# First layer's recurrence: the last sum of the read-out moves from GpSimd and VectorE to TensorE

## The reference

```python
def _step(Sm, inputs):
    q_t, k_t, v_t, beta_t = inputs
    Sk = jnp.einsum('bhde,bhe->bhd', Sm, k_t)
    delta = v_t - Sk
    Sm = Sm + beta_t[..., None] * jnp.einsum('bhd,bhe->bhde', delta, k_t)
    o_t = jnp.einsum('bhde,bhe->bhd', Sm, q_t)
    return (Sm, o_t)
...
return outputs @ Wo + bo
```

## Time and profile before

| | |
|---|---|
| device time, median of 3 runs | 4969.15 us |
| lowest and highest | 4963.04, 4973.53 us |
| span of the profiled execution | 4960.9 us |
| PE / DVE / ACT / POOL busy over the span | 77% / 73% / 51% / 60% |
| PEld busy over the span | 35% |

### The profile page before, as it was taken

How to read it: one execution, slowest core, us unless ns; L and a number is a source line. 1 busy time by engine, 2 the same in 40 slices (tenths; PEclk the granted TensorE clock), 3 DMA queues, 4 the chain that set the end, 5 groups by cost and what they waited for, 6 DMA issues and landing times. The chain is left out here.

```text
span 4960.9 us, 46627 instructions
## 1 busy us (share of the span) xinstructions
PE 3814.6 (77%) x13222; PEld 1745.4 (35%) x13222; DVE 3629.3 (73%) x5288; ACT 2514.6 (51%) x3881; POOL 2956.4 (60%) x2245
## 2 busy tenths in 40 slices
PE   5444565999649978888787799998978777777776
PEld 2111223754226633333333454553423222222222
DVE  7999774134547679999998544545543899999998
ACT  4444431344538856666664344444355555555554
POOL 4888465027254479999993211114420798889987
PEclk7777788999869999999999898989989999899998
DMA  1110211112211144444441432321100444444342
GB/s 50 43 43 9 84 38 55 68 57 76 97 56 58 43 143 156 154 154 157 156 152 62 89 43 38 42 34 48 61 9 34 142 134 141 134 138 140 129 141 98
DMA packets 161698, 434.77 MB, mean 88 GB/s; under 512 B 28150, under 2 KB 51384, under 8 KB 160048
## 3 DMA queue, kind: packets, MB, share of 16 engines
q1 hardware_dynamic: 142512, 374.41, 24.7%
q0 software_dynamic: 18944, 57.57, 3.3%
HBM read 363.67 MB, written 68.68 MB: 87 GB/s over the span
## 5 line engine op out<-in xcount | busy, mean ns | idle before, releaser
L1673 ACT ACTIVATE mb_h<-m_dt,m_a_neg 128x512 f32<-128x512 f32 x1024 | 665.0, 681 | 724.0 <-DVE r L1828 332.8
L1532 PE MATMUL mb_y<-r,m_diag_y 128*128 128x512 f32 x1024 | 546.9, 669 | 275.8 <-POOL r L1753 164.8
L1819 DVE TENSOR_TENSOR_SCAN mb_h<-mb_h,m_u 128x1024 f32<-128x1024 f32 x320 | 734.0, 2294 | 10.4
L1776 POOL TENSOR_TENSOR m_u<-m_bsb,m_xs 128x1024 f32<-128x1024 f32 x256 | 599.9, 2366 | 175.7 <-DMA m_bsb<-bc_rows 175.7
L1776 POOL TENSOR_TENSOR m_u<-m_bsb,m_dtx 128x1024 f32<-128x1024 f32 x256 | 596.2, 2358 | 49.1 <-DVE m_dtx L1860 27.9
L1532 PE MATMUL mb_y<-m_hc,w_common 128*128 128x512 f32 x1024 | 495.3, 623 | 153.3 <-DVE m_hc L1828 87.2
L1819 DVE TENSOR_TENSOR_SCAN m_hs<-mb_h,m_u 128x1024 f32<-128x1024 f32 x192 | 437.5, 2279 | 1.7 <-POOL m_u L1776 1.7
L1532 PEld LDWEIGHTS mb_y<-r,m_diag_y 128*128 128x128 f32 x1024 | 196.1, 207 | 622.2 <-POOL r L1753 244.0
L2302 DVE TENSOR_REDUCE at_mx<-at_ps_s 128x4 f32<-128x512 f32 (+1 forms) x256 | 242.8, 957 | 233.6 <-PE at_ps_s L2116 233.6
L1753 POOL TENSOR_TENSOR r<-m_hs,m_csb 128x1024 f32<-128x1024 f32 x128 | 306.0, 2391 | 119.1 <-DVE m_hs L1819 118.5
L1532 PEld LDWEIGHTS mb_y<-m_hc,w_common 128*128 128x128 f32 x1024 | 190.4, 196 | 450.5 <-issue 191.6
(11 more groups left out here) (518 smaller groups left out, 8519.4 us busy)
## 6 DMA issues: line engine op xcount, KB each, us to landing
m_bsb<-bc_rows SPq DMA_DIRECT2D x256, 512.0 KB, 4.9
m_csb<-bc_rows SPq DMA_DIRECT2D x256, 512.0 KB, 4.0
at_q<-q_parts SPq DMA_DIRECT2D x144, 128.0 KB
x_slots<-d_zeros SPq DMA_DIRECT2D x8, 1024.0 KB, 5.0
kept_x<-r SPq DMA_DIRECT2D x2, 4096.0 KB, 14.1
xg_xg<-x_slots SPq DMA_DIRECT2D x32, 256.0 KB, 2.6
y_slots<-xg_yo POOLq DMA_DIRECT2D x32, 256.0 KB, 2.3
xl_xg<-x_slots SPq DMA_DIRECT2D x32, 256.0 KB, 2.6
```

The source lines that it names most:

```text
L1532: mm = nc.tensor.matmul(ps_y[:, h], weight, hc[:, q % RING, s], start=False, stop=g == GROUPS - 1 and s == SG - 1)
L1673: ins = nc.scalar.activation(ps_h[:, q % 2, s], dt[:, i % 2, h], ACT.Exp, scale=a_neg[:, n:n + 1])
L1776: nc.gpsimd.tensor_tensor(u[:, q % RING], bsb[:, n % RING], dtx[:, i % 2, h].unsqueeze(1).broadcast_to([P, SG, TILE]), ALU.mult).then_inc( ...
L1819: V.tensor_tensor_scan(flat(to), flat(ps_h[:, q % 2]), flat(u[:, q % RING]), 0.0, ALU.mult, ALU.add).then_inc(h_ready, 1)
```

## The change

The addition over the last index goes to TensorE. For each half of a tile, 256 outputs a partition, `sum_terms` issues eight products of the unit matrix (`w["eye"]`, stationary) with a strided view of `sq_q`: the moving operand of product `e` is element `e` of each group of eight, so its neighbouring columns lie eight float32 numbers apart. All eight add up in PSUM, in the bank of `rounding.pst`. `halve` on GpSimd and `outputs` on VectorE are gone, and so is `o_tm` in SBUF. `turn_out` now reads PSUM, and stands after pair 2 of the next tile, where it stood after pair 1. The semaphore `summed` takes the place of `o_part` and `halved`: `queries` waits for it by half tiles, and `turn_out` for both halves.

```diff
-        o_tm = sb("o_tm", [P, TILE])
...
+        o_tm = rounding.pst[:].rearrange("p (m b) c -> p m (b c)", m=2)
...
+            def sum_terms(a, m):
+                pe.wait_ge(sq_ready, a * PAIRS + (m + 1) * PAIRS // 2)
+                if a and m == 0:
+                    pe.wait_ge(o_turned, a)
+                half = STEPS // 2
+                terms = sq_q[:, m * half:(m + 1) * half].rearrange("p t h e -> p (t h) e")
+                for e in range(D0):
+                    mm = nc.tensor.matmul(o_tm[:, m], w["eye"], terms[:, :, e], start=e == 0, stop=e == D0 - 1)
+                mm.then_inc(summed, 1)
...
                 if i:
+                    sum_terms(i - 1, 1)
                     out(i - 1)
                 ffn(i)
+                sum_terms(i, 0)
+            sum_terms(NT - 1, 1)
             out(NT - 1)
...
                 if i:
-                    pool.wait_ge(o_part, (i - 1) * 4 + p // 2 + 1)
+                    pool.wait_ge(summed, (i - 1) * 2 + p // (PAIRS // 2) + 1)
...
-            def halve(i, j):
-                pool.wait_ge(sq_ready, i * PAIRS + 2 * j + 2)
-                both = sq_q[:, 4 * j:4 * j + 4].rearrange("p t h e -> p (t h) e")
-                G.tensor_tensor(both[:, :, 0:D0 // 2], both[:, :, 0:D0 // 2], both[:, :, D0 // 2:], ALU.add).then_inc(halved, 1)
...
-            def outputs(i, j):
-                dve.wait_ge(halved, i * 4 + j + 1)
-                V.tensor_reduce(o_tm[:, j * P:(j + 1) * P], sq_q[:, 4 * j:4 * j + 4].rearrange("p t h e -> p (t h) e")[:, :, 0:D0 // 2],
-                                AX, ALU.add).then_inc(o_part, 1)
...
             def turn_out(i):
-                dve.wait_ge(o_part, 4 * i + 4)
+                dve.wait_ge(summed, 2 * i + 2)
                 if i:
                     dve.wait_ge(o_projected, i)
-                V.transpose(o_fm[:], o_tm[:]).then_inc(o_turned, 1)
+                V.transpose(o_fm[:], rounding.pst[:].rearrange("p m c -> p (m c)")).then_inc(o_turned, 1)
...
-                    if p == 1 and i:
-                        outputs(i - 1, 3)
-                        turn_out(i - 1)
                     if p == 1 and more:
                         norms(i + 1)
+                    if p == 2 and i:
+                        turn_out(i - 1)
...
-                    if p in (3, 5, 7):
-                        outputs(i, p // 2 - 1)
```

More of the change, by code:

```diff
@@ L300, in delta_ffn @@
         (block, projected, evacuated, turned, sqk_ready, norm2, norm1, shifted, rn_ready, parts, m_ready, c_ready, prepared, s_gated,
-         stepped, state_ready, sq_ready, o_part, o_turned, o_projected, s_ready, h_ready, relu_ready, r2_ready, y_ready,
-         g_ready, mixed, lifted, gated, zeroed, cleared, halved, x_in0, x_in1, *rounds) = ctx.enter_context(phase(
+         stepped, state_ready, sq_ready, summed, o_turned, o_projected, s_ready, h_ready, relu_ready, r2_ready, y_ready,
+         g_ready, mixed, lifted, gated, zeroed, cleared, x_in0, x_in1, *rounds) = ctx.enter_context(phase(
              nc, "projected evacuated turned sqk_ready norm2 norm1 shifted rn_ready parts m_ready c_ready prepared s_gated "
-             "stepped state_ready sq_ready o_part o_turned o_projected s_ready h_ready relu_ready r2_ready y_ready "
-             "g_ready mixed lifted gated zeroed cleared halved x_in0 x_in1 "
+             "stepped state_ready sq_ready summed o_turned o_projected s_ready h_ready relu_ready r2_ready y_ready "
+             "g_ready mixed lifted gated zeroed cleared x_in0 x_in1 "
               "round_chain fc_ready fc_turned low1 low1s low2 proj_ready proj_turned round_done"))
@@ L526, in _ @@
                     queries(i, p)
-                    if p % 2:
-                        halve(i, p // 2)
                     if p == 0 and more:
@@ L622, in _ @@
                         turn(i + 1)
-                    if p == 1 and i:
-                        outputs(i - 1, 3)
-                        turn_out(i - 1)
                     if p == 1 and more:
                         norms(i + 1)
+                    if p == 2 and i:
+                        turn_out(i - 1)
                     if p == 2 and more:
                         inverse(i + 1)
-                    if p in (3, 5, 7):
-                        outputs(i, p // 2 - 1)
                     if p == 5 and more:
                         overlaps(i + 1)
-            outputs(NT - 1, 3)
             turn_out(NT - 1)
```

## The result

The changed kernel takes 4989.82 us, the median of 11 runs (4982.19 to 5006.19); the kernel before took 4965.99 us beside it. The ratio is 1.0059, with a 95% interval of 1.0038 to 1.0080: slower by about 29 us, where 4960.2, no measurable change, was forecast. (The medians are 23.8 us apart; the ratio is formed from the fast runs alone, without one of the kernel before at 6565.52 us.) The profiled execution has a span of 4999.2 us.

What follows compares the result with a forecast made beforehand. VectorE was taken to bound the recurrence phase. Removed work -41.3, new waits +28.6 and +0.4, and the phase's end +3.4 sum to -8.9 us: 4960.2 us from 4969.15, eight-in-ten range 4947 to 5004.

Steps and rivals of the forecast that it cites:

- I take the cheap side, as nearest: TensorE's sums: strided columns assumed to cost what columns cost now, 0.214 us an instruction, 3.42 us for eight products.
- rival A: TensorE's sums: strided columns cost twice, eight products take 6.84 us, VectorE waits 5.0 us a tile, 4998.8 us; chance 0.33.
- VectorE's and GpSimd's removed work: Recurrence tiles: 37.8 us off VectorE plus the big transposition's 3.5 us wait for GpSimd, together 41.3 us.
- the place of the wait: VectorE at the small transposition, for sums queued behind TensorE's third and fourth projection: 2.2 us in 13 tiles, 28.6 us.
- the small transposition out of PSUM: VectorE's small transposition reading PSUM instead of SBUF: cost 0, bounds -0.3 and +1.6 us over 16.
- GpSimd's wait at the big transposition: Start of each tile: the big transposition's wait for GpSimd's last product, 0.29 us in each of 12 tiles, would go.
- Rival B: TensorE stays at 2.4 GHz, sums end earlier and VectorE never waits: -39.7 us, 4929.5; chance 0.07.
- Rival C: GpSimd takes over as the bound, with about 21 of 28.5 us a tile; judged impossible, no separate chance given.

Runs made afterwards that it cites:

- e1: Changed kernel with each product reading another buffer at its own stride, output meaningless; 0.216 us an instruction at stride 1, 0.45 to 0.46 at 8.
- e2: Changed kernel with the product buffer's last index outermost, so TensorE reads neighbouring columns; ratio 0.9983 to the kernel before.
- e3: Changed kernel, strided sums kept, with the small transposition one pair later, behind pair 3 and `inverse`; ratio 0.9945 to the kernel before.
- e10: Changed kernel, strided sums kept, with `inverse` and then the small transposition behind pair 3; ratio 0.9931 to the kernel before.
- e6: Kernel before with only the small transposition moved, from behind pair 1 to behind pair 2, ahead of `inverse`; ratio 1.0022 to the kernel before.
- e8: Changed kernel with neighbouring columns, `inverse` and then small transposition behind pair 3, last half's sum split in two; 0.9898 of the kernel before, 4920.1 against 4967.81 us.
- e5: Changed kernel with the second half's sums issued ahead of the third and fourth projection on TensorE; ratio 1.0016 to the kernel before.

## Why the prediction was wrong

*The failed step* is "I take the cheap side, as nearest": 16 x 0.214 = 3.42 us for eight products that read one float32 of eight. They take 16 x 0.46 = 7.4, since a float32 read alone out of its 16 bytes costs 1.8 ns and not 0.84 (e1). Ahead of it stands the reason given, that GpSimd is indifferent to distance. For writing that is still so (e2), but the evidence was from another engine at 2.5 ns a column, and the text itself had noted so: an engine that needs 2.5 ns a column need not show a price of 1.8. The rival had a stated rule behind it, and the forecast nothing of its own: with no nearer row for the cheap end, A deserved at least even chances. The rule of 16-byte lines, cited there against the choice, was the one to follow.

*What followed from it* was rival A: a wait of 5.0 us in 13 tiles (3.6 to 5.4 measured, 4.9 in the mean), 0.8 in tile 15 (1.4), 5.1 more at the end (592.53 - 584.86 = 7.67 us where there were 2.02, so 5.7), and 4998.8 us, +29.6. Measured: +29 us, and 30.1 in the phase. One clause in it was off: the lower level does not double the price again, it stays 0.46 us an instruction.

*The rest held.* VectorE's and GpSimd's removed work, 41.3 us (the period less its wait is 33.4 - 4.9 = 28.5, as forecast); the place of the wait, behind the third and fourth projection; and the small transposition out of PSUM, 716 ns against some 711. e2 is the forecast's own case with the one wrong price put right: -8.8 us of phase against -8.9 forecast, a stall of 2.26 against 2.2, and 37.4 - 7.5 (at the end) = 29.9 us of wait in the tiles against 28.6 + 0.4. GpSimd's wait at the big transposition is gone.

*Rival B* needed TensorE not to fall to 1.2 GHz. In the changed kernel it is still at 1.00 when the third projection starts (333.46) and falls right behind that: 0.52 in the window 334 to 335. e3 and e10 show the rival's case: with the slow sums and almost no wait of VectorE, the mean clock over 200 to 300 us is 1.00, where the changed kernel has 0.91. *Rival C* didn't come: GpSimd is busy 61.5 us of 100. (Its "about 21" is 0.79 x 31.2 - 4 x 1.27 = 19.6 by the rows, which changes nothing.)

*Found only by the runs*: `turn_out`'s new place ahead of `inverse`, costed at nothing, takes 8.0 us by itself where VectorE doesn't wait there (e6). In the changed kernel the wait covered it.

*Left open*: why strides of 16 and 32 are slightly cheaper than 8; and the last 2 us between e8 and e10.

## What to carry to other kernels

When TensorE is to sum over an index, make that index the outermost one of the buffer, so that each matmul reads neighbouring columns, or at least two float32 of every 16 bytes that it touches; the writer (here GpSimd) may pay nothing for the distance. Before a wait is filled by moving its producer forward, try moving the consumer later by one step: the first moved the wait to another engine here (e5), the second removed it (e3). And a short VectorE instruction can be stretched by a GpSimd instruction that began just before it; the profile shows that as a longer busy time, not as a wait, so compare the mean of the same line between versions.

## What was not expected of the hardware

- One MATMUL instruction of a float32 product with 256 columns: 0.216 us at stride 1, 0.33 at 3, 0.43 to 0.46 at 4 and above. At 1.2 GHz the first becomes 0.43 and a stride of 8 stays 0.46, so for strided columns the lower level costs nothing more.
- Two neighbours read out of every eight columns are enough to bring it back to 0.23 to 0.25 us.
- A `TENSOR_SCALAR` of 64 columns took 0.18 us or 0.85, by whether a GpSimd product had begun before it.
- One MATMUL instruction of 64 float32 columns takes as long as one of 128, 0.112 us.
